# Loads of a GNN and mixture-of-experts layer: the matrices in one DMA queue, the experts' parts in another

## The chip, the cores and the metric

The kernel runs on one core of a Trainium2 chip. The metric is the time of one execution on the device, in microseconds (us). Matmuls run on TensorE (PE), vector work on VectorE (DVE), activations and copies on ScalarE (ACT). SyncE (SP) and GpSimd (POOL) issue DMAs here; GpSimd also copies a row over the partitions four times. All DMAs run on the core's 16 DMA engines, whoever issues them.

## The reference, cut to what matters

```python
xn = layernorm(x)                                  # x: (96, 1024) float32
q, k, v = xn @ wq.T + bq, xn @ wk.T + bk, xn @ wv.T + bv
q2, k2, v2 = q @ wiq.T + biq, k @ wik.T + bik, v @ wiv.T + biv   # 16 heads of 64
attn = softmax(q2 k2 / 8 + mask(edges))            # per head, 96 x 96
gnn = (attn v2) @ wo.T + bo
mix = layer_norm(xn + attn_vec(xn @ Wq, xn @ Wkv) @ Wo)   # linear attention, one step long
x = x + gnn + mix
y = layernorm(x)
scores = sigmoid(y @ gate_w.T)                     # 8 experts, the best 2 of each row
h = relu(y * score @ w_up[e].T)**2                 # w_up[e]: (1408, 1024), in bfloat16
routed = sum over the chosen e of h @ w_down[e].T  # w_down[e]: (1024, 1408)
shared = relu(y @ shared_w_up.T)**2 @ shared_w_down.T     # float32
out = x + routed + shared
```

All weights lie in HBM as float32. The first stage has 11 matrices of 1024 x 1024 (4 MB each), the second one shared and eight routed experts with an up and a down matrix each (5.8 MB each). That is some 150 MB to read for 96 rows.

## The kernel before, in words

The 11 matrices of the first stage are read in halves of 512 output columns, 128 partitions x 16 KB, 2048 KB each. They are used in the order of `STEPS`: wq, wk, wv, wiq, wik, wiv, mq, mk, mv with two halves each, then wo 0, mo 0, mo 1, wo 1. The text calls them halves 0 to 21 in that order. `ring` has three places for a half. TensorE works through half c in `out_rows` (line 844 of the profile) and raises `front_done` after its first four tiles and `half_done` after the last: each half has two pieces, and the number of pieces used, `used`, counts them from 1 to 44. When half c is used up, half c + 3 may be read into its place. The three pieces of the shared up matrix (two of 2048 KB, one of 1536 KB) follow in the same ring after half 21, so 22 requests in all are made while TensorE works on the first stage: halves 3 to 21 and shared up 0 to 2.

Beside this stage the first three experts are read. `FIRST_LOADS` cuts each into five parts: the up matrix in three (4, 4 and 3 elevenths), the down matrix in two halves. The text calls them parts 0 to 14. The DMA reads them as float32 and writes bfloat16 into `stage`, so a part moves twice the bytes on the side of HBM that it writes. `FIRST_AT` gives for each the value of `used` at which it is asked for.

SyncE issues the load of x and halves 0 to 2. Everything else of these loads is issued by GpSimd, which waits for the pieces one after the other and issues, at an even `used`, first the half (or piece of shared up) and then a part, if `FIRST_AT` has one there. So all of them go through GpSimd's queue, in the order of the requests. At `used` 36 GpSimd also copies `gamma` over the partitions.

Behind the first stage GpSimd goes on alone: two halves of the shared down matrix (2816 KB each), each when shared pieces are used, then up and down of experts 3 to 6 (2816 KB written each, 5632 KB read) as the three places of `stage` come free, and expert 7 in seven parts. SyncE writes three of the four parts of the output at the end, ScalarE the last.

Of the kernel before, what the change touches and what calls it, by code (L numbers as in the profile page):

```python
# [40 lines left out]
BUF = TT * D  # L41
PIECE = KT * HALF
PIECES = 2
SLOTS = 3
# [20 lines left out]

FIRST_LOADS = [(e, m, x0, x1) for e in range(3) for m, x0, x1 in
               [(0, 0, 4), (0, 4, 8), (0, 8, 11), (1, 0, HALF * TT), (1, HALF * TT, D * TT)]]
FIRST_AT = [0, 3, 6, 9, 13, 16, 21, 24, 29, 32, 37, 39, 42, 44, 44]


MATS = ["wq", "wk", "wv", "wiq", "wik", "wiv", "mq", "mk", "mv"]
STEPS = [(m, h) for m in MATS for h in range(2)] + [("wo", 0), ("mo", 0), ("mo", 1), ("wo", 1)]
# [8 lines left out]
def gps_layer(nc, x, mats, bias_v, bias_o, ln_gamma, ln_beta, edge_rows, columns, shared_up, shared_down, expert_up, expert_down, out):  # L81
    ctx = ExitStack()
    with ctx:
        def sb(name, shape, dt):
            return ctx.enter_context(nc.sbuf_tensor(name, shape, dt))

        def sem(name):
            return ctx.enter_context(nc.semaphore(name))
# [12 lines left out]
        ring = sb("ring", [P, SLOTS * PIECE], F32)  # L101
# [87 lines left out]
        sh_up_landed = [sem(f"sh_up_landed{j}") for j in range(SLOTS)]  # L189
# [74 lines left out]
        def up_before(e):  # L264
            return e * PARTS + PARTS


        def program(engine):
            return lambda written: written(engine)


        def slot_of(c):
            return (c + 2) % SLOTS

        def half_landed(eng, c):
            if c < SLOTS:
                eng.wait_ge(first_landed[c], 16)
            else:
                eng.wait_ge(slot_landed[slot_of(c)], 16 * (c // SLOTS))

        def load_half(eng, c):
            m, h = STEPS[c]
            slot = slot_of(c)
            landed = first_landed[c] if c < SLOTS else slot_landed[slot]
            eng.dma_start(slots[slot], mats[m][h]).then_inc(landed, 16)

        def pieces_used(eng, n):

            if n % PIECES:
                eng.wait_ge(front_done, n // PIECES + 1)  # L290
            else:
                eng.wait_ge(half_done, n // PIECES)

        @program(nc.sync)
        def _(sp):
            sp.dma_start(xs[0:N, 0:D], x).then_inc(x_landed, 16)

            for c in range(SLOTS):
                load_half(sp, c)

            for j, (c0, c1) in enumerate(zip(STORES[:-2], STORES[1:-1])):
                sp.wait_ge(added, DOWN_BEFORE[EXPERTS - 1] + j + 2)
                sp.dma_start(out[:, c0:c1], acc[0:N, c0:c1])\
                  .then_inc(out_landed, 16)
            sp.wait_ge(out_landed, 16 * (len(STORES) - 1))

        @program(nc.gpsimd)
        def _(pool):
            def load(e, m, x0, x1, landed):
                b = e % 3  # L310
                f0, f1 = (x0 * UNIT, x1 * UNIT) if m == 0 else (x0, x1)
                place = stage[b].rearrange("p (m n) -> p m n", m=2)[:, m, :].bitcast(BF16)
                pool.dma_start(place[:, f0:f1], (expert_up, expert_down)[m][e, :, f0:f1])\  # L313
                    .then_inc(landed, 16)

            def load_shared_up(j):
                f0, f1 = j * PIECE, min((j + 1) * PIECE, BUF)
                pool.dma_start(ring[:, f0:f1], shared_up[:, f0:f1]).then_inc(sh_up_landed[j], 16)

            half_landed(pool, 0)
            load(*FIRST_LOADS[0], FIRST_LANDED[0])
            pool.wait_ge(bias_v_landed, 16)
            nc.gpsimd.partition_broadcast(bias_v_b, bias_v_b[0:1, :]).then_inc(spread, 1)
            pool.wait_ge(ln_landed, 16)
            nc.gpsimd.partition_broadcast(beta, beta[0:1, :]).then_inc(spread, 1)
            pool.wait_ge(bias_o_landed, 16)
            nc.gpsimd.partition_broadcast(bias_o_b, bias_o_b[0:1, :]).then_inc(spread, 1)  # L330
            for used in range(1, len(STEPS) * PIECES + 1):
                pieces_used(pool, used)
                if used % PIECES == 0:
                    c = used // PIECES - 1 + SLOTS
                    if c < len(STEPS):
                        load_half(pool, c)
                    else:
                        load_shared_up(c - len(STEPS))
                if used == 36:
                    pool.wait_ge(ln_landed, 32)  # L340
                    nc.gpsimd.partition_broadcast(gamma, gamma[0:1, :]).then_inc(spread, 1)
                for n in range(1, len(FIRST_LOADS)):
                    if FIRST_AT[n] == used:
                        if n == 10:
                            pool.wait_ge(pv_psum, 2)
                            pool.wait_ge(mvec_t_psum, 2)
                        load(*FIRST_LOADS[n], FIRST_LANDED[n])


            for j, (f0, f1) in enumerate([(0, HALF * TT), (HALF * TT, BUF)]):  # L350
                pool.wait_ge(up_done, PARTS - (j == 0))
                pool.dma_start(ring[:, f0:f1], shared_down[:, f0:f1]).then_inc(sh_dn_landed[j], 16)

            for e in range(3, EXPERTS - 1):
                pool.wait_ge(up_done, up_before(e - 3) + PARTS)
                load(e, 0, 0, TT, up_landed[e % 3])
                pool.wait_ge(down_done, DOWN_BEFORE[e - 3] + len(HALVES))
                load(e, 1, 0, D * TT, down_landed[e % 3])
            e = EXPERTS - 1
            pool.wait_ge(down_done, DOWN_BEFORE[e - 3] + len(FINE))  # L360
            load(e, 0, 0, 8, up_landed[1])
            load(e, 0, 8, TT, part_landed[0])
            load(e, 1, FINE_CUTS[0], FINE_CUTS[1], down_landed[1])
            for j in range(1, len(FINE)):
                load(e, 1, FINE_CUTS[j], FINE_CUTS[j + 1], part_landed[j])
# [765 lines left out]
```

## Time and profile before

| | |
|---|---|
| runs | 359.30, 359.33, 361.91 us; median 359.33 us |
| the profiled execution | 357.42 us, its span 356.1 us, so 1.3 us lie around the span |
| TensorE | busy 307.5 us (86%), mean granted clock 0.96 |
| VectorE, ScalarE, GpSimd | busy 111.4, 59.0, 34.2 us |
| DMA | 104.90 MB written, 150.48 MB read from HBM |

The DMA row of the page is the mean busy share of the 16 DMA engines in tenths for 40 equal slices of the span. The GB/s row counts bytes written: where a transfer turns float32 into bfloat16, the bytes read are twice that.

### The profile page before, as it was taken

What the parts mean: (1) busy time and instruction counts of PE and PEld (TensorE: products, weight loads), DVE (VectorE), ACT (ScalarE), POOL (GpSimd) and SP (SyncE); (2) the same over time, 40 slices, a digit from 0 to 9 for tenths busy, and PEclk for the clock granted to TensorE, in tenths of its full rate; (3) what the DMA queues carried; (4) which work ended last, traced back from release to release, by engine and by line L of the source; (5) the groups of instructions that cost most, each with busy time, mean ns of one, the idle gap of its engine ahead of it and who ended that gap; (6) DMA issues with size and microseconds to landing.
All of it is one profiled execution on the core that took longest, in us unless ns stands there. A gap on an engine that the chain in (4) does not pass through costs nothing.

```text
span 356.1 us, 3105 instructions
## 1 busy us (share of the span) xinstructions
PE 307.5 (86%) x1236; PEld 149.9 (42%) x1236; DVE 111.4 (31%) x246; ACT 59.0 (17%) x113; POOL 34.2 (10%) x62
## 2 busy tenths in 40 slices
PE   4999998998999999999959998899998893473674
PEld 4344444333343343433324565543455661241343
DVE  6619436400143439200732312210222330101112
ACT  1410000010003010300020033300223440111131
POOL 0511010110110110211110001000000040000000
PEclk9999999999999999999989999999999996876889
DMA  7999999999999999999999999999999999999997
GB/s 296 387 356 311 395 342 309 353 347 320 431 309 377 393 276 429 265 420 329 307 367 309 211 431 336 218 223 210 225 212 213 225 209 225 213 213 212 209 215 157
DMA packets 8968, 104.90 MB, mean 295 GB/s; under 512 B 1120, under 2 KB 1592, under 8 KB 2812
## 3 DMA queue, kind: packets, MB, share of 16 engines
q0 software_dynamic: 7776, 97.52, 95.0%
q1 hardware_dynamic: 880, 7.05, 5.0%
q10 hardware_dynamic: 300, 0.16, 0.2%
q8 instruction: 8, 0.13, 0.1%
q14 instruction: 4, 0.03, 0.0%
HBM read 150.48 MB, written 0.39 MB: 424 GB/s over the span
## 4 chain that ended last, share of the span: by engine, by line
PE 66%; DMA 26%; DVE 3%; ACT 2%; issue 1%; another core or an unknown queue 1%
PE bank L844 32%; DMA stage<-in_expert_up 14%; PE bank L997 9%; PE bank L1018 9%; PE bank L978 6%; PE bank L1058 5%; DMA ring<-in_mat_wik 4%; DMA ring<-in_mat_mv 4%; DMA ring<-in_mat_wo 4%; PE bank L968 1%; PE bank L815 1%; ACT hbuf L451 1%; PE bank L852 1%; ACT xn L445 1%
## 5 line engine op out<-in xcount | busy, mean ns | idle before, releaser
L844 PE MATMUL bank<-ring,xnt 128*96 128x512 f32 x224 | 99.4, 600 | 0.9 <-ACT xnt L381 0.6
L844 PEld LDWEIGHTS bank<-ring,xnt 128*96 128x96 f32 x224 | 36.3, 165 | 58.8 <-issue 57.7
L1018 PE MATMUL bank<-stage,hbuf 128*96 128x512 bf16 (+5 forms) x242 | 44.0, 341 | 18.1 <-DMA stage<-in_expert_down 14.7
L997 PE MATMUL bank<-stage,hbuf 128*96 128x512 bf16 (+1 forms) x192 | 44.2, 384 | 10.1 <-DMA stage<-in_expert_up 9.6
L844 PE MATMUL bank<-ring,stage 128*96 128x512 f32 x96 | 42.2, 594 | 1.2 <-DMA ring<-in_mat_wik 1.2
L1018 PEld LDWEIGHTS bank<-stage,hbuf 128*96 128x96 bf16 x242 | 26.7, 129 | 33.6 <-issue 18.8
L997 PEld LDWEIGHTS bank<-stage,hbuf 128*96 128x96 bf16 x192 | 24.0, 130 | 26.7 <-issue 14.7
L790 DVE TENSOR_TENSOR acc<-acc_t,acc 96x512 f32<-96x512 bf16 (+5 forms) x22 | 11.9, 542 | 56.2 <-ACT acc_t L470 55.9
L844 PEld LDWEIGHTS bank<-ring,stage 128*96 128x96 f32 x96 | 15.3, 163 | 24.3 <-issue 22.9
L445 ACT ACTIVATE xn<-bank 96x512 bf16<-96x512 f32 (+2 forms) x26 | 14.6, 560 | 65.1 <-PE bank L997 58.8
L777 DVE TENSOR_TENSOR xn<-xn 96x512 bf16<-96x512 bf16 (+1 forms) x24 | 9.6, 399 | 44.6 <-ACT xn L445 44.6
L978 PE MATMUL bank<-ring,xnt 128*96 128x512 f32 (+1 forms) x48 | 21.2, 599 | 0.6 <-ACT xnt L433 0.6
L470 ACT ACTIVATE acc_t<-bank 96x512 bf16<-96x512 f32 (+5 forms) x22 | 10.5, 477 | 52.4 <-PE bank L1018 52.4
L1058 PE MATMUL bank<-ring,xs 128*96 128x512 f32 x44 | 19.0, 592 | 0.0
L580 DVE TENSOR_TENSOR stage<-bank,cols 128x384 f32<-128x384 f32 x10 | 5.5, 556 | 40.6 <-PE bank L852 40.6
L398 ACT ACTIVATE stage<-bank 96x512 f32<-96x512 f32 x10 | 5.9, 593 | 68.9 <-PE bank L844 68.9
L968 PE MATMUL bank<-ident,xn 96*128 96x96 bf16 (+1 forms) x104 | 9.7, 217 | 6.4 <-DVE xn L777 6.4
L313 POOL DMA_DIRECT2D stage<-in_expert_up x15 | 8.1, 543 | 73.0 <-PE bank L997 39.6
L844 PE MATMUL bank<-ring,acc_t 128*96 128x512 f32 x32 | 14.2, 595 | 0.5 <-DMA ring<-in_mat_wo 0.5
L978 PEld LDWEIGHTS bank<-ring,xnt 128*96 128x96 f32 x48 | 8.1, 173 | 11.7 <-issue 10.9
L968 PEld LDWEIGHTS bank<-ident,xn 96*128 96x128 bf16 (+1 forms) x104 | 7.7, 112 | 10.3 <-DVE xn L777 7.5
L1058 PEld LDWEIGHTS bank<-ring,xs 128*96 128x96 f32 x44 | 7.2, 163 | 11.3 <-issue 11.2
(161 smaller groups left out, 192.5 us busy)
## 6 DMA issues: line engine op xcount, KB each, us to landing
stage<-in_expert_up POOLq DMA_DIRECT2D x4, 2816.0 KB, 31.0
stage<-in_expert_down POOLq DMA_DIRECT2D x4, 2816.0 KB, 37.5
stage<-in_expert_down POOLq DMA_DIRECT2D x6, 1408.0 KB, 16.6
stage<-in_expert_up POOLq DMA_DIRECT2D x6, 1024.0 KB, 13.8
ring<-in_shared_down POOLq DMA_DIRECT2D x2, 2816.0 KB, 13.0
ring<-in_mat_wq SPq DMA_DIRECT2D x2, 2048.0 KB, 11.1
ring<-in_mat_wv POOLq DMA_DIRECT2D x2, 2048.0 KB, 12.0
ring<-in_mat_wiq POOLq DMA_DIRECT2D x2, 2048.0 KB, 13.7
```

The source lines that it names most:

```text
L313: pool.dma_start(place[:, f0:f1], (expert_up, expert_down)[m][e, :, f0:f1])\
L398: nc.scalar.activation(plain[h][0:N, :], bank[BANKS[m] + h][0:N, :], ACT.Copy)\
L445: nc.scalar.activation(rows(j), bank[4 + j][0:N, 0:c1 - c0], ACT.Relu)\
L470: nc.scalar.activation(rounded[:, c0:c1], bank[j % 4][0:N, 0:c1 - c0], ACT.Copy).then_inc(out_taken, 1)
L777: tt(r, r, r, ALU.mult).then_inc(h_ready, 1)
L790: tt(acc[0:N, c0:c1], rounded[:, c0:c1], acc[0:N, c0:c1], ALU.add)\
L844: ins = mm(bank[BANKS[m] + h][0:N, :], tiles(src)[:, k, :], w[:, k, :], start=(k == 0), stop=(k == KT - 1))
L968: ins = mm(bank[TURN_BANKS[j]][:, (t - t0) * N:(t - t0 + 1) * N], rows[:, (t - t0) * P:(t - t0 + 1) * P], unit, start=True, stop=True)
L978: ins = mm(bank[4 + j][0:N, 0:c1 - c0], tiles(xnt[:])[:, k, :], w[:, k, :], start=(k == 0), stop=(k == KT - 1))
L997: ins = mm(bank[4 + j][0:N, 0:c1 - c0], tiles(xe)[:, k, :], w[:, k, :], start=(k == 0), stop=(k == KT - 1))
L1018: ins = mm(bank[j % 4][0:N, 0:c1 - c0], tiles(e_h)[:, t, :], w[:, t, :], start=(t == 0), stop=(t == TT - 1))
L1058: ins = mm(bank[j][0:N, 0:c1 - c0], tiles(sh_h)[:, t, :], w[:, t, :], start=(t == 0), stop=(t == TT - 1))
```

## The change

Halves 3 to 21 and the three pieces of shared up are issued by SyncE, in its own loop behind halves 0 to 2: it waits for both pieces of half c - 3 and issues half c, up to the pieces of shared up. GpSimd keeps its loop over `used`, but issues only the parts in it. The moments of the parts change:

| part | 0 | 1 | 2 | 3 | 4 | 5 | 6 | 7 | 8 | 9 | 10 | 11 | 12 | 13 | 14 |
|---|---|---|---|---|---|---|---|---|---|---|---|---|---|---|---|
| `used` before | 0 | 3 | 6 | 9 | 13 | 16 | 21 | 24 | 29 | 32 | 37 | 39 | 42 | 44 | 44 |
| `used` after | 0 | 4 | 9 | 11 | 13 | 18 | 24 | 26 | 27 | 36 | 36 | 37 | 37 | 39 | 40 |

No byte, no tile and no instruction of the compute engines changes.

```diff
-FIRST_AT = [0, 3, 6, 9, 13, 16, 21, 24, 29, 32, 37, 39, 42, 44, 44]
+FIRST_AT = [0, 4, 9, 11, 13, 18, 24, 26, 27, 36, 36, 37, 37, 39, 40]
...
             for c in range(SLOTS):
                 load_half(sp, c)
 
+            def load_shared_up(j):
+                f0, f1 = j * PIECE, min((j + 1) * PIECE, BUF)
+                sp.dma_start(ring[:, f0:f1], shared_up[:, f0:f1]).then_inc(sh_up_landed[j], 16)
+
+            for c in range(SLOTS, len(STEPS) + SLOTS):
+                pieces_used(sp, (c + 1 - SLOTS) * PIECES)
+                if c < len(STEPS):
+                    load_half(sp, c)
+                else:
+                    load_shared_up(c - len(STEPS))
+
...
-            def load_shared_up(j):
-                f0, f1 = j * PIECE, min((j + 1) * PIECE, BUF)
-                pool.dma_start(ring[:, f0:f1], shared_up[:, f0:f1]).then_inc(sh_up_landed[j], 16)
...
             for used in range(1, len(STEPS) * PIECES + 1):
                 pieces_used(pool, used)
-                if used % PIECES == 0:
-                    c = used // PIECES - 1 + SLOTS
-                    if c < len(STEPS):
-                        load_half(pool, c)
-                    else:
-                        load_shared_up(c - len(STEPS))
                 if used == 36:
```

## Rows read from the trace of the kernel before

**Rows 1.** The page: DMA engines and bytes in 40 slices, and the queues.

```profile
DMA  7999999999999999999999999999999999999997
GB/s 296 387 356 311 395 342 309 353 347 320 431 309 377 393 276 429 265 420 329 307 367 309 211 431 336 218 223 210 225 212 213 225 209 225 213 213 212 209 215 157
...
q0 software_dynamic: 7776, 97.52, 95.0%
q1 hardware_dynamic: 880, 7.05, 5.0%
```

**Rows 2.** The waits of TensorE that a DMA ended: us, times, longest.

```profile
PE bank L1018 <- DMA stage<-in_expert_down: 14.7, 5, 6.1
PE bank L997 <- DMA stage<-in_expert_up: 9.6, 2, 6.8
...
PE bank L844 <- DMA ring<-in_mat_wik: 1.2, 1, 1.2
...
PE bank L844 <- DMA ring<-in_mat_wo: 0.5, 1, 0.5
...
PE bank L844 <- DMA ring<-in_mat_mv: 0.2, 1, 0.2
```

**Rows 3.** Busy time in five stretches; the last two columns are DMA share and GB/s written.

```profile
5.00:9.00 4.00, 4.00 (x36) 3.81 (x34) 2.65 (x9) 0.23 (x2) 0.00 (x0) 1.00 1.03 429
14.00:24.00 10.00, 10.00 (x24) 3.75 (x23) 4.11 (x24) 0.61 (x2) 3.79 (x5) 1.00 1.01 323
25.00:28.00 3.00, 3.00 (x25) 1.87 (x24) 1.43 (x8) 0.59 (x1) 0.53 (x1) 1.00 0.99 426
...
240.00:300.00 60.00, 48.91 (x269) 28.63 (x268) 14.22 (x27) 15.43 (x33) 5.83 (x11) 0.97 1.01 216
```

**Rows 4.** GpSimd in order of time: when requests of the ring were issued.

```profile
41.67 0.53 POOL L285 DMA_DIRECT2D ring<-in_mat_wiq  x1 [6.14 <-PE bank L844]
...
103.38 0.53 POOL L285 DMA_DIRECT2D ring<-in_mat_mk  x1 [7.11 <-PE bank L844]
...
111.95 0.53 POOL L285 DMA_DIRECT2D ring<-in_mat_mk  x1 [7.51 <-PE bank L844]
...
118.81 0.53 POOL L285 DMA_DIRECT2D ring<-in_mat_mv  x1 [6.34 <-PE bank L844]
...
148.01 0.53 POOL L285 DMA_DIRECT2D ring<-in_mat_mo  x1 [6.74 <-PE bank L844]
...
200.21 0.54 POOL L352 DMA_DIRECT2D ring<-in_shared_down  x1 [19.69 <-PE bank L978]
...
215.19 0.53 POOL L313 DMA_DIRECT2D stage<-in_expert_up  x1 [7.53 <-PE bank L997]
```

**Rows 5.** DMA issues at those seven moments, in that order: KB, us to landing.

```profile
ring<-in_mat_wiq POOLq DMA_DIRECT2D x1, 2048.0 KB, 11.4
...
ring<-in_mat_mk POOLq DMA_DIRECT2D x1, 2048.0 KB, 12.0
...
ring<-in_mat_mk POOLq DMA_DIRECT2D x1, 2048.0 KB, 11.9
...
ring<-in_mat_mv POOLq DMA_DIRECT2D x1, 2048.0 KB, 9.9
...
ring<-in_mat_mo POOLq DMA_DIRECT2D x1, 2048.0 KB, 13.5
...
ring<-in_shared_down POOLq DMA_DIRECT2D x1, 2816.0 KB, 13.1
...
stage<-in_expert_up POOLq DMA_DIRECT2D x1, 2816.0 KB, 18.0
```

**Rows 6.** DMA issues of the first 3 us, at 10 us and at the end.

```profile
ring<-in_mat_wk SPq DMA_DIRECT2D x1, 2048.0 KB, 23.0
xs<-in_x SPq DMA_DIRECT2D x1, 384.0 KB, 4.0
...
stage<-in_expert_up POOLq DMA_DIRECT2D x1, 1024.0 KB, 14.5
...
out<-acc SPq DMA_DIRECT2D x1, 78.0 KB, 1.6
```

**Rows 7.** TensorE around half 16, in order of time.

```profile
133.15 7.03 PE L844 MATMUL bank<-ring,xnt 128*96 128x512 f32 x16
140.38 1.93 PE L844 MATMUL bank<-ring,xnt 128*96 128x512 f32 x4 [0.20 <-DMA ring<-in_mat_mv]
```

## The prediction, made before the change was run

> **What bounds the kernel now.** I read the page's slices first. The 16 DMA engines are busy nine tenths or more in every slice but the first and the last [rows 1]. TensorE has 86% too, so the question is which of the two has slack. The waits answer it. In the first stage (up to 178 us) TensorE waits for a DMA three times, 1.9 us together. In the second it waits 24.3 us [rows 2]. So in the second stage DMA sets the end, and TensorE could be later by some microseconds without moving it. The stretches then show that the DMA engines are at one rate, whatever they do, if bytes are counted on the side of HBM. Halves alone from SyncE's queue: 429 GB/s. Halves alone from GpSimd's: 426. Casting transfers alone: 216 written, 432 read [rows 3]. Total bytes by that rate, 150.48 MB / 430 GB/s = 350 us, is the stretch from the first transfer at 2 us to the last landing at 352 us. No DMA time is idle, so nothing in this kernel gets shorter except idle DMA time, of which there is none, and the last 4 us. The change can only add idle time or change the rate.
>
> **The price of one request.** At 430 GB/s a half or a 2048 KB piece takes 4.9 us (2.10 MB). A part of up with four elevenths is also 2.10 MB read: 4.9 us. Three elevenths: 3.7 us. Half of a down matrix, 2.88 MB read: 6.7 us. A whole matrix of an expert: 13.4 us.
>
> **How the two queues share.** Part 0 was issued at 10 us and landed 14.5 us later. Half 2 was issued at 2.1 us and landed after 23.0 us, both near 25 us [rows 6]. So both moved side by side between 14 and 24 us, the one from GpSimd's queue and the other from SyncE's. The stretch shows 323 GB/s written [rows 3]. With equal turns for rows of 16 KB read, two thirds of the written bytes are the half's and one third the part's, which counts double at HBM: 323 x 4/3 = 431 GB/s. Equal turns explain the row, and sharing costs nothing there. The bounds of its price are the other rows, 426 to 432, so up to 1.4% either way. I take 431 against 432, 0.2%, over the about 100 us in which both queues will hold work: 0.2 us, ends -1.4 and +1.4.
>
> **Part by part, the issue.** 22 requests of 0.53 us leave GpSimd and go to SyncE. SyncE has nothing else until 350 us, and its stores come behind the loop, whose last wait ends near 179 us. No request is late for its engine: 0. On GpSimd a part no longer stands behind a half. At `used` 36 parts 9 and 10 stand behind the copy of gamma, 1.3 us, and the transposes that part 10 waits for. In FIFO order a half came behind every part asked for earlier. Now it starts at once, at half speed while a part moves: 9.8 us beside an up part, and beside a down part 4.9 x (1 + 6.7/4.9) = 11.6 us. TensorE takes 7.0 us for one. Three places in the ring give about two such steps of lead.
>
> **What the new moments do to the work outstanding.** DMA never idles as long as something is asked for. What is owed just before a request is issued is its time to landing minus its own price, as before is first come, first served. From that I take the parts that the new list has not asked for yet. The four thin places:
> - `used` 8 at 41.7 us [rows 4]: 11.4 - 4.9 = 6.5 us owed [rows 5], part 2 (3.7) is postponed: 2.8 us.
> - `used` 24 at 103.4: 12.0 - 4.9 = 7.1, part 6 (4.9) is only now asked for: 2.2 us.
> - `used` 26 at 112.0: 11.9 - 4.9 = 7.0, part 7 (3.7): 3.3 us.
> - `used` 36 at 148.0: 13.5 - 4.9 = 8.6, part 9 (6.7): 1.9 us.
>
> Elsewhere it is over 4 us. After `used` 36 the new list is ahead of the old one, by 8.6 to 17.1 us of work, and at 44 they are equal. A gap opens where what is owed is shorter than the delay from issue to first byte. The small store of 78 KB, with 0.2 us of bytes, took 1.6 us in all, the load of x 4.0 us with 0.9 us of bytes [rows 6]. The delay lies between 1 and 3.1 us. I take 1.6, from the store, as it has nothing else beside it. With 1.6 none of the four places opens by itself. With 3.1 they would open by 0.3, 0.9, 0 and 1.2 us, 2.4 us together.
>
> **Where TensorE becomes late.** Half 15 is asked for at 112.0 us, with 3.3 us owed and part 7 (3.7) issued in the same moment, all in the other queue in the worst case. Sharing, half 15 is through at 112.0 + 9.8 = 121.8. Half 16 is asked for at 118.8 and starts there. It has 2.1 us of part 7 beside it, which takes both to 126.0, then part 8 (issued at `used` 27, near 115) beside its last 2.8 us: 2.8 x (1 + 6.7/4.9) = 6.6, so 132.6, and with the 1.6 us 134.2. Before, it landed at 118.8 + 9.9 = 128.7 [rows 4, 5], and TensorE began with it at 133.15 [rows 7]. So a wait of about 1.1 us, ends 0 and 2.6 (with 3.1 us). Halves 9 to 11 stand beside parts 4 and 5 and may wait another 0.5 us each, of which 1.2 us is there today [rows 2].
>
> A later TensorE asks later. At `used` 36 its 1.1 us take what is owed from 1.9 to 0.8 us, under the 1.6 us of delay: 0.8 us of idle DMA. In the second stage the shortest stock is at 215.2 us, 18.0 - 13.4 = 4.6 us, and 13.1 - 6.7 = 6.4 at 200.2 [rows 4, 5]. A delay of TensorE of 1 to 3 us is swallowed there. Expert 0 to 2's parts and shared up are in time: the parts are asked for earlier at the end, and each piece of shared up needs at most 11.6 us, with 11 to 22 us until its use.
>
> **The sum.** Idle DMA at `used` 36: 0.8. Small gaps at the other three places, between 0 and 1.2: 0.3, since halves 9 to 11 make the first of them a bit later. Sharing: 0.2. Together +1.3 us on the execution of 357.42 us, 358.7 us. The profiled execution lies 1.9 us under the median of 359.33, so the forecast of the median is 360.6 us. A measurement here tells about 1%, 3.6 us, from no change. The forecast is within that.
>
> **The rivals.**
> - *Halves starve, slower.* If turns go against the halves, because a down part's rows are longer than in the one stretch that the trace shows, or because a request needs 3 us to start, TensorE falls behind. Its cost decides from 4.6 us of delay at 215 us on, where the stock ends; every microsecond beyond is one of idle DMA. With 3.1 us of delay the gaps give 2.4, and waits of some 2.5 us at each of halves 9 to 11 and 16 make 10 us of lateness, 5 more beyond the stock of 4.6. That is +4 to +8, middle 365 us. For it: the wait for half 9 is there today, so this place has no lead. Against it: at 14 to 24 us the half got its full share. 0.19.
> - *No gap opens.* The stock of 1.9 us at `used` 36 holds, TensorE's wait is under 0.3 us: the same time, 359.3 us. For it: 2.8, 2.2 and 3.3 us are all over 1.6. 0.30.
> - *The queue of SyncE is faster.* A rate of 429 against 426 GB/s [rows 3] over the 46 MB moved, 107 us, is 0.7 us: 358.6 us. For over 1% the halves would have to run at 445 GB/s, which no stretch shows. The Trainium skill, "DMA: Bandwidth & Descriptors", Latency and other measured facts, names two DMA engines as usually slower under GpSimd's queue, by contention for its descriptor rings, which SyncE's queue doesn't have. By that rule the moved loads would gain. The mean share of the engines here stays at 1 in both queues, so the trace shows no such loss. 0.09, of which 0.04 for over 1% faster.
> - *The forecast*, 359.9 to 362.9 us: 0.42.
>
> **How the numbers follow.** The four cases give 1.00. The range takes in the slower end of the rival as far as 364.5, where 0.1 is left out, and 358.5 below. Faster by over 1%: 0.04. Slower by over 1% (above 362.9): 0.19 from the starving halves. Within: 0.77.
>
> **What the profile would show.** Right: the queue named hardware dynamic at 30% of the bytes' time or more, DMA slices at 9 everywhere in the middle, at most 2 us of missing DMA share near 149 us, a wait of TensorE for `ring<-in_mat_mv` of about 1 us near 133 us, the waits for the experts shorter by as much as TensorE is late, and the last landing 1 to 2 us later. The step on the stock is wrong if DMA shows gaps at 42, 103 or 210 us. The step on sharing is wrong if a half beside a part takes clearly over 12 us, or if TensorE reaches the end of the first stage later than 183 us. The forecast as a whole fails if bytes move at another rate in mixed stretches than 426 to 432 GB/s at HBM.

## The result, and the profile after

The changed kernel takes 367.17 us (median of four runs, 365.03 to 369.61) against 359.31 us: 1.023 of the time before, 95% interval 1.0195 to 1.0269. The forecast was 360.6 us, with a range to 364.5. A second set of runs gave 1.015 (1.008 to 1.022). The profiled execution took 367.75 us with a span of 366.5 us, 10.4 us over the span before. Its runs lie 4.6 us apart, those of the kernel before within 2.6 us. A ratio leaves out runs over 1.5% above the fastest of their kernel and the medians here do not, so a ratio need not be the quotient of two medians.

The page of the changed kernel: the DMA engines, the granted clock, bytes written and the queues, to be held against [rows 1].

```profile
PEclk9999999989999998999987999999999996768899
DMA  8999999999999999789999999999999999999997
GB/s 301 376 367 344 355 293 329 306 335 389 346 352 309 335 294 413 268 302 280 321 327 314 262 327 429 213 224 214 219 216 216 216 216 220 216 216 213 204 214 160
...
q0 software_dynamic: 4608, 51.91, 63.3%
q1 hardware_dynamic: 4048, 52.67, 35.2%
```

The bytes moved to the other queue as the diff says. The slices at 147 to 165 us fall to 7 and 8, where before every slice in the middle was at 9. The stretches of the changed kernel at three thin places of the prediction (those of 41.7, 103.4 and 148.0 us), then one behind a wait of TensorE:

```profile
43.00:53.00 10.00, 10.00 (x28) 4.02 (x27) 3.19 (x4) 0.59 (x1) 0.53 (x1) 1.00 0.93 289
104.00:110.00 6.00, 6.00 (x43) 2.99 (x42) 3.25 (x6) 0.00 (x0) 0.53 (x1) 1.00 0.93 341
147.00:159.00 12.00, 12.00 (x64) 5.65 (x63) 2.51 (x6) 1.40 (x4) 1.70 (x2) 1.00 0.72 249
76.00:81.00 5.00, 4.98 (x8) 1.84 (x9) 0.00 (x0) 0.00 (x0) 0.00 (x0) 0.66 0.99 324
```

The last two columns are DMA share and GB/s. The missing shares are 0.7, 0.4 and 3.4 us of idle DMA. The column before these two is the granted clock; it is at 0.66 in the fourth row, where TensorE had just waited. Its waits for halves in the changed kernel, to be held against [rows 2]:

```profile
PE bank L845 <- DMA ring<-in_mat_mv: 2.9, 1, 2.9
PE bank L845 <- DMA ring<-in_mat_wik: 2.0, 1, 2.0
PE bank L845 <- DMA ring<-in_mat_mk: 0.9, 1, 0.9
...
PE bank L845 <- DMA ring<-in_mat_wo: 0.2, 1, 0.2
```

They are halves 16, 8, 15 and 21. TensorE in order of time around half 8, the half after it, and half 16:

```profile
76.02 8.78 PE L845 MATMUL bank<-ring,stage 128*96 128x512 f32 x16 [1.99 <-DMA ring<-in_mat_wik]
...
84.97 7.03 PE L845 MATMUL bank<-ring,stage 128*96 128x512 f32 x16
...
140.93 15.64 PE L845 MATMUL bank<-ring,xnt 128*96 128x512 f32 x32 [2.88 <-DMA ring<-in_mat_mv]
```

Half 8 took 8.78 us in place of 7.0, and halves 16 and 17 took 15.64 us where three halves in a row take 20.84, so 13.9 for two. Behind each of these two waits the granted clock was at 1.2 GHz for a while, which cost about 1.8 us on top of the wait. GpSimd's copy of gamma, issued when half 17 is used up, shows how late TensorE was: 156.86 us, before 148.57 us.

Where the bytes fell behind can be read from the trace's records of the DMA rows. I counted the bytes on the side of HBM and took, at moments of the kernel before, how much later the same number had been moved (us). How the bytes of a row are spread over its time moves single numbers by 0.1 to 0.4. This table carries most of what follows:

```
moment in the kernel before    50    96   108   143   155   201   213   225   339
changed kernel                2.0   2.7   4.5   4.7  10.2  10.1  10.4  10.4  10.3
queue change alone            0.3   0.6   0.7   1.6   1.8   1.7   3.0   4.7   4.6
moments alone                 1.4   1.6   3.8   3.7   9.2   8.8  19.3  20.7  20.9
part 9 earlier                1.9   2.4   4.2   4.6   4.5   4.4  10.7  12.5  12.4
half rows                     2.3   3.2   3.2   3.6   3.8   3.9   4.3   4.4   4.5
half rows, old moments        0.3   0.8   0.8   1.2   1.5   1.6   2.1   2.1   2.0
busy waits                    2.2   2.7   3.8   4.0   7.0   7.0   7.3   7.1   7.3
late TensorE, one queue       0.1   0.4   0.5   2.0   2.1   3.1   6.1   7.9   7.9
half rows, one queue          0.0   0.1   0.2   0.3   0.3   0.2   0.6   0.7   0.6
old moments, busy waits      -0.1   0.1   0.2   1.2   1.3   1.3   1.9   2.8   2.9
first eight moments old      -0.1   0.1   0.2   0.3   2.9   2.9   3.2   3.3   3.4
```

The changed kernel loses 10.3 us in the first stage and nothing after it: some 1.7 us near 45 us, 1.8 near 106, 5.5 between 148 and 158, and 1.3 in small steps. All of the difference of the spans, 10.4 us, is in this row.

### The profile page after: what moved, and what is told of

Read it like the earlier page. It is cut to its first block, busy times and chain, and to the rows that moved or that the text cites. A ratio compares the mean times of both kernels' runs of the same rounds, so it can differ in the third digit from the quotient of the medians.

```text
span 366.5 us, 3110 instructions
## 1 busy us (share of the span) xinstructions
PE 314.7 (86%) x1236; PEld 152.5 (42%) x1236; DVE 111.2 (30%) x246; ACT 59.0 (16%) x113; POOL 22.3 (6%) x40
## 4 chain that ended last, share of the span: by engine, by line
PE 67%; DMA 24%; DVE 4%; ACT 2%; issue 1%; another core or an unknown queue 1%; DVEq 0%
PE bank L845 34%; DMA stage<-in_expert_up 13%; PE bank L998 8%; PE bank L1019 8%; PE bank L979 6%; DMA ring<-in_mat_wik 5%; DMA ring<-in_mat_mv 5%; PE bank L1059 5%; ACT hbuf L452 1%; PE bank L816 1%; PE bank L969 1%; PE bank L831 1%; PE bank L853 1%; ACT xn L446 1%
## 5 line engine op out<-in xcount | busy, mean ns | idle before, releaser
L845 PE MATMUL bank<-ring,xnt 128*96 128x512 f32 x224 | 102.2, 614 | 4.4 <-DMA ring<-in_mat_mv 2.9
L845 PEld LDWEIGHTS bank<-ring,xnt 128*96 128x96 f32 x224 | 37.1, 169 | 64.3 <-issue 63.2
L998 PE MATMUL bank<-stage,hbuf 128*96 128x512 bf16 (+1 forms) x192 | 45.3, 390 | 9.8 <-DMA stage<-in_expert_up 9.3
L845 PE MATMUL bank<-ring,stage 128*96 128x512 f32 x96 | 43.8, 612 | 2.0 <-DMA ring<-in_mat_wik 2.0
L791 DVE TENSOR_TENSOR acc<-acc_t,acc 96x512 f32<-96x512 bf16 (+5 forms) x22 | 11.9, 542 | 56.0 <-ACT acc_t L471 55.7
L979 PEld LDWEIGHTS bank<-ring,xnt 128*96 128x96 f32 x48 | 8.2, 177 | 12.1 <-issue 11.2
L969 PEld LDWEIGHTS bank<-ident,xn 96*128 96x128 bf16 (+1 forms) x104 | 7.7, 112 | 10.3 <-DVE xn L778 7.5
L1059 PEld LDWEIGHTS bank<-ring,xs 128*96 128x96 f32 x44 | 7.2, 163 | 11.3 <-issue 11.2
```

The lines of the kernel that those rows point to most:

```text
L791: tt(acc[0:N, c0:c1], rounded[:, c0:c1], acc[0:N, c0:c1], ALU.add)\
L845: ins = mm(bank[BANKS[m] + h][0:N, :], tiles(src)[:, k, :], w[:, k, :], start=(k == 0), stop=(k == KT - 1))
L969: ins = mm(bank[TURN_BANKS[j]][:, (t - t0) * N:(t - t0 + 1) * N], rows[:, (t - t0) * P:(t - t0 + 1) * P], unit, start=True, stop=True)
L979: ins = mm(bank[4 + j][0:N, 0:c1 - c0], tiles(xnt[:])[:, k, :], w[:, k, :], start=(k == 0), stop=(k == KT - 1))
L998: ins = mm(bank[4 + j][0:N, 0:c1 - c0], tiles(xe)[:, k, :], w[:, k, :], start=(k == 0), stop=(k == KT - 1))
L1059: ins = mm(bank[j][0:N, 0:c1 - c0], tiles(sh_h)[:, t, :], w[:, t, :], start=(t == 0), stop=(t == TT - 1))
```

## The experiments

Unless said otherwise a ratio is to the kernel before on the same chip, with its 95% interval. The median of before was 358.01 us for the first four kernels, 358.26 for the next four and 358.12 for the last four.

**The queue change alone.** The changed kernel with the old list.

```diff
-FIRST_AT = [0, 4, 9, 11, 13, 18, 24, 26, 27, 36, 36, 37, 37, 39, 40]
+FIRST_AT = [0, 3, 6, 9, 13, 16, 21, 24, 29, 32, 37, 39, 42, 44, 44]
```

> The queue change alone: halves and shared up from SyncE, the parts at the old moments. Theory (a half that shares the DMA engines with a part lands late, TensorE waits for it and then runs at the lower clock, is late at its next requests, and the DMA engines run dry): the old moments put more parts beside the halves, so TensorE waits as long as in the changed kernel or longer (5 to 8 us in the first stage), but more work is outstanding, so less DMA time is idle: 2 to 6 us slower than before, 361 to 365 us. Rival, the new moments are the cause: with the old ones the time is that of before, 359.3 us, with waits of TensorE under 2 us in the first stage. Rival, loads from SyncE's queue move at a lower rate: as slow as the changed kernel, 366 us or more, with DMA slices full.

Measured 366.62 us (362.82 to 368.24), 1.0225 (1.017 to 1.028). The rival that the moments are the only cause falls. The profiled run, the fastest, waits 3.2 us for half 9 and 1.5 for half 17, is 3.2 us late at the copy of gamma (151.77 us) and loses 4.6 us of bytes, nearly 3 of them at 201 to 225 us in the second stage. Behind the long wait the clock did not fall. Of half 9's 16 matmuls the first 15 take 6.65 us, 0.44 us each as in a half of 7.0 us:

```profile
83.73 6.65 PE L845 MATMUL bank<-ring,stage 128*96 128x512 f32 x15 [3.25 <-DMA ring<-in_mat_wik]
```

The third rival, a slow rate with full slices, would show a steady loss; the row has 1.7 us of it by 201 us.

**The moments alone.** The kernel before with the new list, in one queue.

> The new moments alone, everything in GpSimd's queue as before. Theory: the new moments leave little work outstanding at 42, 103 and 148 us, and in one queue a half also stands behind the whole part asked for ahead of it, so TensorE waits for half 16 and for later ones and DMA is idle for 5 us or more: slower than the changed kernel, 368 to 376 us. Rival, the second queue alone is the cause: then the time is that of before, within 1 us of 359.3 us.

Measured 381.88 us (378.98 to 383.78), 1.066 (1.061 to 1.071). As expected in sign, worse than expected. With one queue half 21 stands behind parts 9 to 12, 11.4 us of wait, and the DMA engines then stand still. The stretch of the second stage in this kernel:

```profile
213.00:225.00 12.00, 12.00 (x56) 6.80 (x55) 4.20 (x14) 1.25 (x3) 0.53 (x1) 1.00 0.28 100
```

A DMA share of 0.28 over 12 us is 8.6 us without work. So each edit is bad without the other as well, and the new list needs the second queue.

**Part 9 earlier.** The changed kernel with part 9 at `used` 33.

```diff
-FIRST_AT = [0, 4, 9, 11, 13, 18, 24, 26, 27, 36, 36, 37, 37, 39, 40]
+FIRST_AT = [0, 4, 9, 11, 13, 18, 24, 26, 27, 33, 36, 37, 37, 39, 40]
```

> The changed kernel with part 9 asked for at used 33 in place of 36, so that the DMA engines have work in the stretch from 148 to 159 us where they ran dry (some 3 us of missing share there). Theory: the idle time there goes, 2 to 3 us come back, about 364.5 us, unless it only returns in the second stage, where TensorE is still 9 us later than before. Rival, idle DMA is a symptom and the rate of mixed stretches the cause: no change, 367 us.

Measured 369.43 us, 1.032 (1.027 to 1.037), slower than the changed kernel by about 1%. Two stretches of this kernel:

```profile
147.00:159.00 12.00, 12.00 (x64) 5.68 (x63) 1.38 (x3) 3.11 (x5) 2.49 (x4) 1.00 1.00 314
208.00:224.00 16.00, 15.50 (x71) 9.30 (x70) 4.25 (x9) 2.47 (x5) 1.06 (x2) 1.00 0.66 259
```

The gap at 148 us is filled, share 1.00, and 5.4 us of idle DMA stand at 208 to 224 us instead. The part also shared with the halves behind it: TensorE waited 5.0 us for the two halves of mo and 2.0 for wo, besides 3.2 for the two of wik and 1.6 for half 16. A filled gap gives nothing as long as TensorE is late: the work asked for behind the first stage comes later by its lateness.

**Half rows.** The changed kernel; each of the 15 parts is two DMAs of half the columns, so its rows are half as long. TensorE waits for the first ones' semaphore before each of the three experts.

```diff
+                if e < 3:
+                    fm = (f0 + f1) // 2
+                    pool.dma_start(place[:, f0:fm], src[e, :, f0:fm]).then_inc(first_halves[e], 16)
+                    f0 = fm
```

> The changed kernel with each of the 15 parts asked for as two DMAs of half the columns, so that a row of a part is half as long and the half beside it gets two turns' worth of bytes for one (if the DMA engines take turns by rows): a half beside an up part would take 7.4 us of transfer in place of 9.8. Theory (the share is what makes the halves late): the waits of TensorE for halves 8, 15 and 16, 5.8 us together, fall under 2 us, and the time to 361 to 363 us. Rival (turns go by something else than rows, or the lateness comes from the moments): waits and time stay as in the changed kernel, 367 us.

Measured 361.04 us (359.94 to 363.56), 1.009 (1.005 to 1.013). This is the clearest test: no moment and no queue differs from the changed kernel, only the length of the parts' rows (and with it the number of their requests, which the one-queue control below prices). The waits of TensorE for halves:

```profile
PE bank L850 <- DMA ring<-in_mat_wo: 0.8, 1, 0.8
PE bank L850 <- DMA ring<-in_mat_mo: 0.6, 1, 0.6
PE bank L850 <- DMA ring<-in_mat_wiv: 0.2, 1, 0.2
```

1.6 us in place of 6.0. The gap at 148 us is gone, that at 45 us is still there (2.3 us by 50 us). The row records show the turns directly: from 95 to 102 us the two queues began 123 rows of halves and 112 of parts, the latter with half the bytes, and where one row begins as another ends, rows of the two queues mostly alternate one by one. The ratios show it less sharply than the waits: the changed kernel had 1.023 and, beside the second set of versions, 1.015 (1.008 to 1.022), which overlaps with this interval. In the medians the gain is 4.3 to 6.1 us.

**Half rows, old moments.** The same with the old list.

> Two queues, each part as two DMAs of half the columns, and the parts at the old moments. Theory: the halves come in time through their larger share and the stock of work is the old one, so no DMA time is idle in the middle; what is left over the kernel before is only the slightly longer rows where both queues move (624 against 611 ns for a row of a half, some 2 us in all): 1.0 to 2.5 us over before. Rival (a second queue costs by itself): 5 us or more over before, as with the queue change alone.

Measured 359.79 us (359.48 to 360.97, ten runs), 1.005 (1.003 to 1.007): 1.5 us over before, inside what the theory gave, without a gap anywhere. What is left grows in small steps to 2.0 us. It is the price of the second queue as such. In the row records the median row of a half takes 624 ns where a part moves in the other queue, here and in the changed kernel, against 611 ns in one queue. All bytes at HBM from 30 to 180 us moved at 425.5 GB/s here, at 430.5 in the kernel before and at 429.0 with half rows in one queue.

**Half rows in one queue**, the control.

> The kernel before with each part as two DMAs of half the columns, all in GpSimd's queue: the control for the two kernels with half rows. Theory: shorter rows cost and give nothing by themselves, within 1 us of before. Rival: they cost 1 us or more, and what they gave with two queues was more than was seen.

Measured 358.52 us, 1.001 (0.998 to 1.003). Short rows neither cost nor give as much as 1 us.

**Busy waits.** The changed kernel with matmuls whose results nothing uses ahead of three halves.

```diff
+                for _ in range({8: 2, 15: 1, 16: 3}.get(c, 0)):
+                    mm(bank[BANKS[m] + h][0:N, :], tiles(xnt[:])[:, 0, :], xnt[:, 0:HALF], start=True,
+                       stop=True)
                 half_landed(pe, c)
```

> The changed kernel with 2, 1 and 3 matmuls of 0.86 us, whose results nothing uses, ahead of halves 8, 15 and 16 on TensorE, where it waited 2.0, 0.9 and 2.9 us. Theory (each wait costs about 1.9 us more through the lower clock behind it, and these microseconds come back as idle DMA): the clock stays at 2.4 GHz through the first stage, TensorE is 3 to 4 us earlier at its end, and the time falls by 2 to 4 us, to 363 to 365 us, with less spread over the runs. Rival (the clock is a by-product): no change or slower.

Measured 366.15 us (364.27 to 367.96), 1.022 (1.016 to 1.028). In its profile:

```profile
76.00:81.00 5.00, 5.00 (x13) 1.89 (x12) 0.00 (x0) 0.00 (x0) 0.00 (x0) 1.00 0.98 326
141.00:146.00 5.00, 5.00 (x14) 1.81 (x13) 4.93 (x3) 0.00 (x0) 0.00 (x0) 1.00 1.00 429
```

The clock stays at 1.00 in both stretches, the copy of gamma comes at 153.73 in place of 156.86 us, and the loss of bytes is 7.3 in place of 10.3 us. So in the profiled executions the clock's part is about 3 us. The medians, 366.15 against 367.17 and 365.34 for the two sets of the changed kernel, don't show it. Here the theory's time was not confirmed.

**The changed kernel again.**

> The changed kernel once more, beside the others on this chip: 1.018 to 1.028 of before. Each theory expects the same; it shows how far its runs lie apart, and whether the one with the higher mean clock is the faster.

Measured 365.34 us (361.18 to 368.37), 1.015 (1.008 to 1.022). The fastest run had clock 0.957, the others 0.948 and 0.949. In the first set the run with clock 0.958 was the fastest too (365.03), but one with 0.953 the slowest (369.61). The profiled run (368.37) shows the same picture as the first: waits of 2.9, 2.3, 0.9 and 0.2 us for the same halves and a loss of 10.8 us of bytes, counted as in the table.

**Late TensorE, one queue.** The kernel before with 5 such matmuls ahead of half 8 and 5 ahead of half 16; no load is changed.

> The kernel before, one queue, old moments, with 5 matmuls of 0.86 us that nothing uses ahead of half 8 and 5 ahead of half 16: TensorE is made 8.6 us late without any change to a load. Theory (lateness costs from the point where it is over the stock of 4.6 us at 215 us): some of the idle DMA time comes at 210 to 215 us, and the time is 3 to 6 us over before. Rival (TensorE has slack enough in the second stage, lateness is harmless, and the changed kernel is slow by its DMA rate): within 1 us of before.

Measured 365.63 us (365.0 to 367.31), 1.0205 (1.016 to 1.025), 7.4 us over before. The rival falls: 8 us of lateness alone, in one queue and with the old list, cost as much as the whole change. It costs more than the theory gave, too. The first request of the second stage came 8.0 us late, and the stretch behind it shows 1.2 us of idle DMA in four:

```profile
208.23 0.53 POOL L352 DMA_DIRECT2D ring<-in_shared_down  x1 [21.52 <-PE bank L981]
```

```profile
207.00:211.00 4.00, 4.00 (x24) 2.84 (x23) 1.79 (x3) 0.59 (x1) 0.53 (x1) 1.00 0.71 171
```

The loss of bytes is 7.9 us at the end, practically all of the lateness. A stock of 4.6 us, as I had worked it out, swallowed next to nothing.

**Old moments, busy waits.** The queue change alone with 3 such matmuls ahead of half 9 and 1 ahead of half 17.

> The queue change alone with matmuls of 0.86 us that nothing uses, 3 ahead of half 9 and 1 ahead of half 17, where TensorE waited 3.2 and 1.5 us. Of the four runs of the queue change alone the one with clock 0.957 took 362.8 us, those with 0.943 and 0.948 took 366 to 368. Theory (the waits let the clock fall in most runs, and that makes TensorE late past the stock): all runs near 362 to 364 us. Rival (the spread has another cause): median near 366 us again.

Measured 361.52 us (360.38 to 363.19, six runs), 1.009 (1.005 to 1.012). TensorE's waits for halves fall to 1.5 us. Against the queue change alone (366.62 us in the first set, 365.16 on this chip) that is 5.1 and 3.6 us, by work that does nothing but fill a wait. What went away are the longest runs: the fastest of the queue change alone on this chip, 360.35 us, is as fast as the fastest here. That it is the clock is not shown: the profiled run of the first set waited 3.2 us without a fall of the clock, and its copy of gamma came at 151.77 us, against 151.14 here.

**First eight moments old.** The changed kernel with parts 1 to 7 at the old moments.

```diff
-FIRST_AT = [0, 4, 9, 11, 13, 18, 24, 26, 27, 36, 36, 37, 37, 39, 40]
+FIRST_AT = [0, 3, 6, 9, 13, 16, 21, 24, 27, 36, 36, 37, 37, 39, 40]
```

> The changed kernel with parts 1 to 7 at their old moments, parts 8 to 14 at the new ones. Theory (idle DMA comes where the list leaves too little outstanding): the losses near 44 us (2.1 us) and 106 us (1.9 us) go, the one near 148 to 158 us stays (5 us), so about 3 to 4 us under the changed kernel unless TensorE gets later, 362 to 365 us. Rival (the losses follow from TensorE's lateness alone): all of them stay, 366 us or more.

Measured 362.69 us (361.08 to 364.99), 1.0135 (1.009 to 1.018). The losses at 45 and 106 us are gone as expected. The one at 148 us is 2.6 us in place of 5.5, since TensorE was only 1.3 us late there (copy of gamma at 149.90 us). The idle time belongs to the list, its size to the lateness. TensorE's one long wait, 3.3 us for half 9, was again not followed by a fall of the clock.

**The queue change alone, again.**

> The queue change alone once more, beside the version with busy waits on this chip: median 364 to 367 us, and slower the lower the mean clock of the run.

Measured 365.16 us against 358.12, four runs from 360.35 (clock 0.962) to 368.31 (clock 0.934), too far apart for an interval. The order by clock was as expected at both ends and not between them (365.94 us had 0.958, 364.38 had 0.953). In the profiled run (364.38) TensorE waited 1.9 us for half 9, and this time the clock fell behind it: the half took 8.78 us.

## Why the prediction was wrong

- **What bounds the kernel** held. DMA was full before, only idle time and rate could change, and the loss of bytes is the difference of the spans, 10.3 of 10.4 us. The second stage ran at the same rate as before. The signs that the prediction named against its own steps came: gaps near 45 and 106 us, a half beside a part that takes 14.4 us, and the last request of the first stage at 186.8 us, past 183.
- **The price of sharing** was mis-sized: +0.2 us, with an end of +1.4. Half rows with old moments, where nothing is idle, measured +1.5 us in time and 2.0 us in bytes. The 431 GB/s for the stretch of 14 to 24 us was worked out from equal turns; counted row by row, the same stretch of the kernel before moves 426.6 GB/s at HBM, 0.9% under its 430.5 elsewhere. So the price could be read before the change.
- **The stock of work** is the step that failed first. I took time to landing minus the price of the request as the work ahead, and asked whether it is over 1.6 us of delay. The four places were found rightly; three of them lost 1.7 to 1.8, 1.8 and 5.5 us where I had 0.3 for the small ones and 0.8 for the last. Time to landing is the time of the last of 16 DMA engines. In the kernel before, the first and the last engine through with a request are 1.2 to 1.4 us apart (the 4-byte rows that each writes at its end), so the stock was that much smaller. The delay was too short for parts as well. In the changed kernel SyncE's half at 149.74 us moved its first row 1.0 us later, but parts asked for at 46.70, 85.37, 106.97 and 157.99 us began after 2.0, 3.7, 4.2 and 3.9 us. This stood in the trace before the change: part 0, issued at 9.96 us, moved its first row at 13.85 us, 3.9 us later, and its queue was empty. The 1.6 us came from a plain store of SyncE. And after a gap the first rows take 0.8 to 2.1 us instead of 0.61.

  From kernels with lateness in one place one can work back what the quantity of the prediction must be for no loss. At 200.2 us it was 6.4. In late TensorE the request came 8.0 us late, the bytes 3.1, so 6.4 - 4.9 = 1.5, and 3.0 us were lost by 213 us: some 4.5. The queue change alone (4.7 late, the bytes 1.7, 1.3 lost) and old moments with busy waits (3.8 late, the bytes 1.3, 0.6 lost) give 4.7 and 4.5. With the first eight moments old, 1.9 - 1.0 = 0.9 at 148 us and 2.6 lost: some 3.5. By 3.5 to 4.5 in place of 1.6 all four places of the new list were too thin from the start. The bound is an estimate, worked back from two places; how delay, spread and slow first rows add up to it is not shown.
- **Half 16's wait** was +1.1 us (0 to 2.6). It was 2.9 us, with 0.9 and 2.0 more for halves 15 and 8, for which I had nothing. I had let half 15 begin at 112 us, all owed work being in the other queue. In fact it was asked for at 115.0 us, TensorE being late, and half 14 was still ahead of it in its own queue: the queue of halves moves at half speed as a whole, so halves 14, 15 and 16 landed 8.7 and 11.3 us apart (halves 6, 7 and 8 some 12.5), and TensorE uses one in 7. These are SyncE's requests for halves 14, 15 and 16 of the changed kernel, each from a view of its moment:

```profile
ring<-in_mat_mk SPq DMA_DIRECT2D x1, 2048.0 KB, 14.4
...
ring<-in_mat_mk SPq DMA_DIRECT2D x1, 2048.0 KB, 14.5
...
ring<-in_mat_mv SPq DMA_DIRECT2D x1, 2048.0 KB, 18.9
```

  Before, the same three took 12.0, 11.9 and 9.9 us [rows 5]. Part of the rest is the spread of the engines. First and last engine through with a half, from the trace's 4-byte rows (us):

```
half                      7            8           11           14           15           16
changed kernel   58.7-63.1   71.2-75.6   93.8-97.9  115.5-120.5  126.0-129.2  136.8-140.4
```

  3.2 to 5.0 us, against 1.2 to 1.4 before. These six are the widest of the changed kernel, its others have 3.0 at most. What opens the spread is not shown: two queues alone do not, the halves of half rows with old moments have 0.3 to 1.9. TensorE waits for the last engine.
- **The clock** was no term at all. In the changed kernel each of the two longer waits cost 1.8 us more at the lower clock, and busy waits removed it in the profile, with 3 us of bytes. The length of a wait does not decide it: the clock fell behind waits of 1.9 to 2.9 us (changed kernel twice, its repeat twice, the second queue change alone), and not behind 3.2 (the first queue change alone), 3.3 (first eight moments old) or 2.3 and 2.7 us (part 9 earlier). When it falls stays open.
- **The swallowing of lateness in the second stage**: "a delay of TensorE of 1 to 3 us is swallowed there". It was not. The queue change alone came to the second stage with TensorE 3.0 us further behind than its bytes (4.7 against 1.7) and lost 3.0 us there; late TensorE in one queue lost 7.9 us in all for 8.0 us of lateness. The size at which lateness starts to cost was the same mistaken stock.
- **The rivals.** The case that came in time was the first, halves starve (+4 to +8, 0.19): its mechanism and its middle, 365 us, are near what was measured. Its price was worked from 3 us of delay; the runs put a short stock, the spread of the engines and the clock in that place. Turns did not go against the halves: with rows of equal bytes they got half, with the parts' rows halved they came in time.
- The Trainium skill's "DMA: Bandwidth & Descriptors", Latency and other measured facts, has two engines usually slower and gives GpSimd's queue as its best guess at the cause. No run gained from moving loads off that queue: half rows with old moments is 0.5% slower, not faster. That rule showed no effect here.

How the parts add up in the changed kernel's profile: 1.7 and 1.8 us at the first two thin places, 5.5 at the third, 1.3 of steady loss. Of the 5.5, 2.6 came with TensorE nearly in time (first eight moments old), the rest with its 8.3 us of lateness, of which the busy waits take back about 3 in bytes.

Open is why the runs of kernels in which TensorE waits in the first stage lie up to 8 us apart (queue change alone, 360.35 to 368.31 us over both sets), those without such waits 1.5 us (half rows, old moments). The clock goes along with it at the ends, but not run by run, and the busy waits lowered the median in one of two pairs. The two profiles of the queue change alone show the wait for half 9 with and without a fall of the clock behind it, which would spread the runs, but only one execution of each set was profiled.

No version beat the kernel before. Its DMA engines are never idle between the first load and the last, so there was nothing to win by an order of loads.

## What to carry to other kernels

Where the DMA engines are full at one rate, as here, a reordering has nothing to win and can lose. Compare the work outstanding at each request with the delay to the first row, plus the spread between the DMA engines, plus the lateness of the engine that asks; here 3.5 to 4.5 us of "time to landing minus price" were needed.

A second queue takes the first-come order away. The urgent queue moves at its share of turns as a whole, and if the background transfers must lie beside it, shorter rows for them give it a larger share (1.023, or 1.015 in the second set, fell to 1.009 by that alone).

A wait of 2 to 3 us on TensorE can cost nearly 2 us more behind it, though several as long cost nothing more, and every microsecond by which the consumer is late can come back as idle DMA.

## What was not expected of the hardware

- Turns go by single rows: halving the rows of one queue's transfers cut TensorE's waits on the other queue from 6.0 to 1.6 us with nothing else changed, and cost nothing in one queue (1.001).
- The 16 DMA engines can drift apart: up to 5.0 us between the first and the last for a half of the changed kernel, 1.2 to 1.4 in one queue, at most 1.9 for the halves of half rows with old moments.
- A casting transfer from GpSimd began 3.7 to 4.2 us after its issue for three of the parts looked at, 2.0 for a smaller one; a plain load from GpSimd began after 1.2 us (issued at 213.64 us in part 9 earlier, first row at 214.88), a half from SyncE after 1.0.
- After a gap of 1 to 2 us the first rows of 16 KB took 0.8 to 2.1 us in place of 0.61.
- The granted clock fell behind waits of TensorE of 1.9 to 2.9 us and stayed up behind others of 2.3 to 3.3 us.
